# A graph layer's sum over source nodes: from accumulating scatters to a sort by node tile and a second pass

## The reference

```
h = x @ W_w + W_b
row, col = src, dst
e = leaky_relu(h[row] @ a_src + h[col] @ a_dst + a_b)
attention = softmax(e)                      # over all edges
out = segment_sum(attention * h[col], row)  # by the source node
```

## Time and profile before

| | us |
|---|---|
| median of three runs | 7000.66 (6996.76 to 7005.89) |
| time of the profiled execution | 7027.32 |
| its span, first to last instruction | 7025.2 |

### The profile page before, as it was taken

The page is one execution under the profiler, slowest core; times in us unless marked ns, Lnnn a source line. Parts: engine busy times, 40 slices in busy tenths (PEclk is TensorE's granted clock), DMA queues, the critical chain, the costliest instruction groups (busy, mean ns, idle before and its releaser), DMA issues. The chain is left out here.

```text
span 7025.2 us, 105591 instructions
## 1 busy us (share of the span) xinstructions
PE 3688.3 (53%) x22271; PEld 3019.6 (43%) x22272; DVE 3433.4 (49%) x9812; ACT 1300.7 (19%) x2255; POOL 3820.9 (54%) x3356
## 2 busy tenths in 40 slices
PE   3444454424444444444434444444445777777776
PEld 3444444424434434433323333333334555555554
DVE  4433444378633334333365555555574444444456
ACT  1111111136622222222220000000022111111111
POOL 3655666510078888888805555555514555555550
PEclk7767667665555555555566666666677989888888
DMA  4322233206765555555543333333323444444441
GB/s 101 83 78 80 82 83 81 80 13 173 209 102 86 87 88 87 87 86 87 71 119 93 94 93 93 92 94 94 93 82 103 125 123 123 124 125 125 121 119 56
DMA packets 673487, 691.12 MB, mean 98 GB/s; under 512 B 103982, under 2 KB 540746, under 8 KB 673324
## 3 DMA queue, kind: packets, MB, share of 16 engines
q0 software_dynamic: 230080, 341.66, 23.3%
q1 hardware_dynamic: 443372, 349.06, 18.1%
HBM read 598.62 MB, written 91.71 MB: 98 GB/s over the span
## 5 line engine op out<-in xcount | busy, mean ns | idle before, releaser
L1054 POOL DMA_INDIRECT acc<-R,a_idx x832 | 1313.5, 1579 | 270.1 <-issue 195.8
L1318 POOL DMA_INDIRECT X<-table_ps,r_idx x832 | 822.7, 989 | 879.1 <-DVE r_idx L1371 634.2
L1129 POOL DMA_INDIRECT R<-table_kv,h_idx x832 | 818.4, 984 | 811.2 <-DVE h_idx L1182 573.1
L565 POOL DMA_INDIRECT R<-table,c_idx x832 | 812.6, 977 | 564.2 <-DVE c_idx L610 285.0
L996 PE MATMUL psum<-R,a_oht 128*128 x2496 | 353.4, 284 | 839.6 <-DVE a_oht L962 828.9
L590 PE MATMUL psum<-c_msg,c_oh 128*128 128x128 f32 x1664 | 364.1, 387 | 706.8 <-remote 601.4
L1414 DVE TENSOR_TENSOR R<-R,psum 128x256 f32 x832 | 346.8, 417 | 794.6 <-remote 514.9
L1335 PE MATMUL psum<-w_L_gnn_re_w,r_ea 128*128 128x256 f32 x1664 | 580.9, 431 | 266.4 <-DVE r_oht L1379 197.7
L996 PEld LDWEIGHTS psum<-R,a_oht 128*128 128x128 bf16 x2496 | 259.6, 104 | 953.5 <-issue 897.5
L590 PEld LDWEIGHTS psum<-c_msg,c_oh 128*128 128x128 f32 x1664 | 312.8, 281 | 755.5 <-issue 666.6
L1156 PE MATMUL psum<-h_msg,h_oh 128*128 128x137 f32 x1664 | 366.1, 383 | 377.5 <-DVE R L1236 242.6
(11 more groups left out here) (255 smaller groups left out, 6920.2 us busy)
## 6 DMA issues: line engine op xcount, KB each, us to landing
R<-in_ea_t SPq DMA_DIRECT2D x832, 64.0 KB
R<-src_rows SPq DMA_DIRECT2D x208, 256.0 KB
r_ea<-in_ea_t SPq DMA_DIRECT2D x832, 64.0 KB
R<-rel_rows SPq DMA_DIRECT2D x104, 256.0 KB
R<-lo_rows SPq DMA_DIRECT2D x104, 256.0 KB
a_rel<-rel_rows SPq DMA_DIRECT2D x208, 128.0 KB
h_rel<-rel_rows SPq DMA_DIRECT2D x208, 128.0 KB
r_rel<-rel_rows SPq DMA_DIRECT2D x208, 128.0 KB
```

The lines of the kernel that those rows point to most:

```text
L565: g.indirect_dma_start(out=rows[:, u, :], out_offset=None, in_=table, in_offset=bass.IndirectOffsetOnAxis(ap=idx[:, u:u + 1], axis=0)).the ...
L1054: g.indirect_dma_start(out=accs[u % ACCS], out_offset=bass.IndirectOffsetOnAxis(ap=idx[:, u:u + 1], axis=0), in_=out_rows[:, u, :], in_off ...
L1129: g.indirect_dma_start(out=rows[:, u, :], out_offset=None, in_=table, in_offset=bass.IndirectOffsetOnAxis(ap=idx[:, u:u + 1], axis=0)).the ...
L1318: g.indirect_dma_start(out=rows[:, u, :], out_offset=None, in_=table, in_offset=bass.IndirectOffsetOnAxis(ap=idx[:, u:u + 1], axis=0)).the ...
```

## The change

The sum by `src` is made in two passes.

- `phase_tables` keeps `hi_rows`, the source's node tile of each slot by rows, or -1 for a slot that counts for nothing. In `phase_conv_edges` DVE counts, one node tile in each turn, how many such slots each step has (L661 to L666 of the new kernel), and ACT issues 208 transfers that fill a new HBM table `by_src` of 832 x 128 rows of 130 floats with zeros and a very low score.
- `phase_order` makes running sums of the counts on PE and DVE, so that each pair of step and node tile gets its first place in `by_src`; each node tile begins at a multiple of 128. The places go through HBM in three digits.
- `phase_permute` replaces `phase_scores_edges` and the first half of `phase_attend`: for eight steps at a time PE also finds each slot's place (L958 on) and expands `h[dst]`; ACT copies the rows to SBUF, unscaled, and DVE adds the score and the source inside the tile as columns 128 and 129; POOL writes the 128 rows of each step to their places, without an addition; slots that count for nothing get an index beyond the table and are dropped.
- `phase_softmax` needs fewer steps. `phase_attend` becomes the second pass: SP loads four tiles of `by_src` at a time, ACT makes the weights (exp), POOL makes a one-hot matrix with the weight in it for each tile, PE multiplies, DVE adds into the node tile in SBUF.
- `phase_attend_nodes` loads nothing; `Norm` is rewritten with `bn_stats` in 50 small instructions and a last step split 34 to 16 between DVE and ACT. Some buffers are placed elsewhere.

```
@@ Norm
-        link(v.tensor_reduce(mean, Y, AX.X, ALU.add))
...
-            v.tensor_tensor(OUT[:, cut, :], Y[:, cut, :], wide(var, cut), ALU.mult).then_inc(self.done, 1)
+            for t in range(cut.start, cut.stop):
+                ins = v.bn_stats(self.stats[:, t, :], Y[:, t, :])
...
+            for t in range(cut.start, cut.start + self.ON_VECTOR):
+                ins = v.tensor_scalar(OUT[:, t, :], Y[:, t, :], self.mean[:, t:t + 1], self.root[:, t:t + 1],
+                                      ALU.subtract, ALU.mult)
...
+            for t in range(cut.start + self.ON_VECTOR, cut.stop):
+                ins = self.nc.scalar.activation(OUT[:, t, :], Y[:, t, :], ACT.Identity, bias=self.shift[:, t:t + 1],
+                                                scale=self.root[:, t:t + 1])
@@ phase_conv_edges
+                        nc.scalar.dma_start(filled[:, bass.ds(i * U + j * G, G), :],
+                                            k.fill[:].unsqueeze(1).to_broadcast([P, G, ROW])).then_inc(fill_done, 16)
                         a.wait_ge(summed, GROUPS * i + j + 3)
...
+                    if j == 0:
+                        v.tensor_scalar(same_high[:], k.hi_rows[:], k.lane[:, bass.ds(i, 1)], None, ALU.is_equal).then_inc(matched, 1)
...
+                        v.tensor_reduce(k.count[:, :, bass.ds(i, 1)], same_high[:], AX.X, ALU.add).then_inc(counted, 1)
@@ phase_order
+                for j in range(SB):
+                    pe.matmul(of(j), k.earlier[:], count16[:, j, :], start=True, stop=(j == 0))
+                    for b in range(j):
+                        pe.matmul(of(j), k.ones16[:], count16[:, b, :], start=False, stop=(b == j - 1))
...
+                link(v.tensor_tensor_scan(upto, tiles_f, nought, 0.0, ALU.add, ALU.add))
...
+                for n in range(3):
+                    sp.dma_start(k.digit_dram[n].rearrange("(j p) h -> p j h", p=P),
+                                 digit[:, n, :].rearrange("p (j h) -> p j h", h=NT)).then_inc(stored, 16)
+                sp.wait_ge(table_known, 1)
...
+                    sp.dma_start(k.order_dram[0].rearrange("(j p) -> p j", p=P), table).then_inc(kept, 16)
+                sp.wait_ge(kept, 16)
+                sp.dma_start(k.order[0:1, :], k.order_dram[0:1, :]).then_inc(got, 16)
@@ phase_permute, scalar
+                def copy(i, j):
...
+                        for u in range(G8 * j, G8 * j + G8):
+                            a.wait_ge(row_out[u], 16 * i)
...
+                        nc.scalar.copy(rows[:, G8 * j + G * h:G8 * j + G * h + G, 0:D],
+                                       k.psum[:, 4 + 2 * j + h, :].rearrange("p (q d) -> p q d", d=D)).then_inc(rows_ready, 1)
@@ phase_permute, tensor
+                    pe.matmul(k.psum[:, 2 + j, 0:G8 * NT], k.earlier[:], mask[:, j, :, 0:NT], start=True, stop=False)
+                    pe.matmul(k.psum[:, 2 + j, 0:G8 * NT], k.worth[0:3, :], digits[0:3, j, :],
+                              start=False, stop=True).then_inc(placed_done, 1)
...
+                pipeline(pe, ITERS, PER, place, score, expand, lags=(0, 0, 0))
@@ phase_permute, gpsimd
+                with g.Fori(0, ITERS) as i:
+                    for u in range(U):
+                        n = PER * i + u // G8
+                        if u % G8 == 0:
+                            g.wait_ge(ready, n + 1)
+                        if u % G == 0:
+                            g.wait_ge(rows_ready, 2 * n + u % G8 // G + 1 + 2 * PER)
+                            g.sem_inc(pool_turn, 1)
+                        g.indirect_dma_start(out=by_src, out_offset=bass.IndirectOffsetOnAxis(ap=idx[:, u:u + 1], axis=0),
+                                             in_=rows[:, u, :], in_offset=None,
+                                             bounds_check=STEPS * P - 1, oob_is_err=False).then_inc(row_out[u], 16)
@@ phase_attend
+                        sp.wait_ge(product, SLOTS * i + g + 1)
+                        sp.dma_start(ring[:, g * G:(g + 1) * G, :], tiled[:, bass.ds((SLOTS * i + g) * G, G), :]
...
+                        for q in range(G):
+                            ins = p.tensor_scalar(oh[:, g, q, :], k.lane[:], ring[:, g * G + q, D + 1:D + 2], weight[:, g, q:q + 1],
+                                                  ALU.is_equal, ALU.mult)
+                        ins.then_inc(oh_ready, 1)
...
+                        for q in range(G):
+                            mm = pe.matmul(k.psum[:, g, q * D:(q + 1) * D], oh[:, g, q, :], ring[:, g * G + q, 0:D],
+                                           start=True, stop=True)
...
+                        if g * G % U == 0:
+                            node = load_steps(nc, v, k.order, (SLOTS * i + g) * G, NT - 1)
+                        v.wait_ge(product, n + 1 + SLOTS)
...
+                            v.wait_ge(added, G * n + q + SLOTS * G)
+                            v.tensor_tensor(agg[:, t, :], agg[:, t, :], k.psum[:, g:g + 1, q * D:(q + 1) * D],
+                                            ALU.add).then_inc(added, 1)
@@ phase_attend_nodes
-                for n in range(ACCS):
-                    v.wait_ge(landed[n], 16)
-                    link(v.tensor_tensor(Y, Y, bufs[n] if n else k.X[:], ALU.add))
+                link(v.scalar_tensor_tensor(out=Y, in0=agg, scalar=k.soft[:, 5:6], in1=k.X[:], op0=ALU.mult, op1=ALU.add))
```

587 lines of the change are left out of this document (336 added, 251 removed).

## The result

The changed kernel takes 7136.3 us (median of four runs, 7128.2 to 7150.0), the kernel before in the same comparison 6999.7 us: a ratio of 1.0182, with a 95% interval of 1.0166 to 1.0199. It is slower by 1.8%, where 6700 us and "faster" were forecast. The profiled execution of the changed kernel has a span of 7138.4 us.

The account below looks back on a forecast made before the run. Each stage had its own limit, the sum by source POOL's issue (1584 us). 7027.3 - 312 (replaced stages) - 24 (norms) + 35 (first layer) + 8 (marking) = 6734; median 6707, said 6700; range 6610 to 6960.

Parts of the forecast that it names:

- The price of the scatter: Permute: each plain scatter keeps POOL busy 1.0 us with 0.325 us idle between two, 1102 us for 832.
- The first rival: Permute: the plain scatter costs POOL what the adding one does, 1584 us, kernel at 7180; chance 0.12.
- So POOL hides the rest: Permute: other engines' work for eight steps, at most 10.2 us, fits under POOL's 10.6; stage 1117 us.
- a ring with 5 us to spare: Permute: landing and copies must fit into POOL's 10.6 us for the other eight steps, leaving some 5 us.
- The second rival: Second pass: waits called remote come back as in the first layer, 250 us more, kernel at 6950; chance 0.10.
- The second pass: Second pass: DVE and PE at its lower clock level at 442 us, POOL just under; stage 470 us.
- the third rival: Second pass: POOL bounds it from 0.53 us an instruction; at 0.8 us 670 us, kernel at 6900; chance 0.10.
- Accumulators and norm, order, softmax: Stages around permute and second pass: accumulators' stretch with norm 32 us, order chain 32 us, softmax 13 us.
- The norms: Rewritten norms: 21 us each, 8 less; three outside the replaced stages save 24 us.
- The first layer: First layer's edges: DVE's counting, a third of 85 us showing, and some for ACT's filling transfers, +35 us.
- Marking: Marking of slots ahead of the first layer's edge loop and in the tables: +8 us.
- Slower: Whole kernel slower than before, through the first rival or a mixture of two others; chance 0.14.

Follow-up runs that it names:

- the quick chip: One of three chips, where four runs fell; the kernel before took 5838 us there, against 7013 to 7035 us on the other two.
- split kernel: Changed kernel with DVE making one of each group's four one-hot matrices in the second pass: 7057 us (1.0029) on one chip, 6987 us (0.9952) on another.
- the relatives: Changed kernel with a 64-column memset before each scatter (5681 us), an eighth of SP's permute loads (5660), or scatters writing nothing (5675), beside 5838 us.
- the run without data: Changed kernel with all scatter indices beyond the table's end, so nothing is written: 5675 us beside 5838 us for the kernel before, permute 1097 us.

## Why the prediction was wrong

*The price of the scatter* (1.0 us and 0.325 us between two): right, 0.984 and 0.35. The first rival, the adding price, is out.

*"So POOL hides the rest"* is the step that failed: the overlap of POOL's scatters with the other engines' work. It rested on adding up the other engines' work for eight steps, at most 10.2 us against POOL's 10.6, and on a ring with 5 us to spare. The work was even overestimated: without the scatters the whole stage takes 598 us, 5.8 us for eight steps. Nor was the ring too short: with it the quick chip reaches POOL's pace. The failing assumption was that the instructions of one engine cost the same whatever POOL does. Under a row of scatters each 1.28 us apart, PE's do not; the ring then runs dry, and POOL waits 334 us for rows. 281 us of the error are here. On the quick chip, where the assumption holds, the stage takes 1089 to 1105 us, against 1117 forecast. Without these 281 us the kernel would be at an estimated 7138 - 281 = 6857 us, faster than before; so this step alone turned the sign.

The sign of it stood in the rows. The earlier trace rows has 589 and 288 us of waits called remote in the first layer; the prediction says "I do not know what that is; it matters below", and then lets it matter only as a cover for DVE's counting and as a rival in the second pass. The right question would have been what the stages with such waits have in common: plain indirect transfers 1.25 us apart. The sum by source has them 1.85 us apart and no such waits. The change turns 1.85 into 1.28.

*The second rival, remote waits in the second pass*: they didn't come, as its last argument against had it ("no gathers run beside the second pass").

*The second pass*: the third rival came true, to which I had given 0.10. The term mis-sized is POOL's one-hot matrix: 784 ns measured, at the end of the bounds (0.27 to 0.8) and not at the 0.45 taken. The stage: 655 us, 670 predicted for that case. The earlier trace rows gave 2.13 ns a column, 0.27 us; the other 0.51 us are in no row of before. How much of them is start-up is not shown; the memsets of 64 and 256 columns (178 and 337 ns) leave an estimated 0.13 us for it in that form. The Trainium skill's GPSIMD Engine Reference, performance pitfalls, would have made it an estimated 0.44; the measurement is 0.784, so two such reads do not explain it. PE has 431 us of work there. The split kernel's 497 us hold all that DVE does, 82 us of it for the fourth matrix, so its adds and tables fit into 415 us, and the 442 us that I gave them were not too few.

*Accumulators and norm, order, softmax*: 30, 26 and 13 us for 32, 32 and 13. *The norms*: the last one's stretch went from 41 us to 32, the first layer's from 30 to 22.5; 8 us each were forecast. Twenty-five `bn_stats` of 128 columns take 4.93 us, 0.20 us each (0.22 taken).

*The first layer*: +28 for +35, and little of it is certain. *Marking*: 3 us for 8.

*Slower* had 0.14, from the adding price and a mixture. The case that came is POOL bounding the second pass, which was the third rival, together with the permute's cover failing, which was none: it stood only among the signs to look for, with the short ring as its cause. With its two terms, 6734 + 281 + 185, less the 60 us or so by which other stages came out under their terms or moved by themselves, one is at the 7138 us measured. On the quick chip the relatives come out 157 to 178 us below the kernel before, where 300 were forecast: the 185 us of the second pass are missing there too.

What stays open: why one chip is free of it, what in the start of a transfer does it, and what the 0.7 us are. The Trainium skill's page on the runtime (Runtime: NRT & Kernel Launch, instruction fetch mechanics) says that each engine's sequencer fetches its instructions by a DMA queue of its own and that this is mostly hidden. Slow fetching would fit that PE, SP and ACT crawl together, without a semaphore to name. The trace speaks against it. It does list packets of the kind instruction: 13 and 26 in its two queues over the whole changed kernel, and as many in the run without data on the quick chip. In the permute's 1398 us of the changed kernel there is a single one:

```profile
q8 instruction: 1, 0.02, 0.0%
```

As far as these packets are all the fetching by DMA that there is, the loops run without it, and the slow stretches have another cause. Which one stays open.

## What to carry to other kernels

Before an argument of the form "engine X sets the pace and hides the rest", look for a stage that already runs X at that density and see whether the others keep their speed there; idle time put down to issue or remote has a cause, even where the profile names none. A cheaper instruction on the pacing engine can raise the density of what disturbs the others: try a gap before you trust a gain. And price a small POOL instruction by one of its own size, not by the slope of a long one.

## What the runs showed of the hardware

- Plain indirect transfers on POOL, 1.25 to 1.28 us apart, slow the issue of PE, SP and ACT on all chips used but one: PE idle from issue for 481 to 513 us ahead of one line in a stage of 1400 us, and 184 SP instructions of 0.65 to 0.75 us there; ACT idle from issue for 254 us in the first layer of the kernel before and 12 us in the same layer on the quick chip. Accumulating ones, 1.85 us apart, do not (10.8 us, and 1 such SP instruction), and plain ones 1.86 us apart hardly do (8). Writing no data changes nothing (1413 us against 1412).
- On these chips 0.28 to 0.34 us of other work on POOL ahead of each transfer makes the stages shorter: 1412 to 1341 us, and 4.3% for the whole kernel before (0.957).
- On one chip none of this occurred: the kernel before took 5838 us there (one execution) instead of 7013 to 7035, with the same instructions. Spacing by waits is a loss there: 832 transfers with waits for the landing of the third before took 1212 us for some 1100. A memset of 64 columns hid (1105 us); the longer ones were not run there.
- Times on POOL: plain scatter of 128 rows 984 ns, adding scatter 1579 ns (144 packets each, the plain one 32), a memset of 64, 192 and 256 columns 178, 276 and 337 ns, a `tensor_scalar` with two scalars a partition on 128 columns 784 ns (DVE: 395 ns). A scatter lands 2.3 us after its issue.
